# A message-passing layer on one core: node groups inside the message steps, window halves, and a message's last addition on GpSimd

## The chip, the core and the metric

The kernel runs on 1 core of one Trainium2 chip. The metric is the device time in microseconds, the median of 3 runs: 1063.25 us before the change (1062.73 to 1063.36).

## What is computed

50,000 nodes with 128 features, 50,000 edges sorted by target node, 32 edge types, 8 base matrices:

```python
h = jnp.maximum(_layernorm(x, axis=-1), 0.0)
W_rel = jnp.einsum('rb,bdf->rdf', w_comp, weight)
seg = etype * n_nodes + dst
agg = jax.ops.segment_sum(h[src] * norm, seg, num_segments=n_rels * n_nodes)
agg = agg.reshape(n_rels, n_nodes, d_in)
node_repr = jnp.einsum('rnd,rdf->nf', agg, W_rel)
node_repr = node_repr + h_bias + h @ loop_weight
return x + jax.nn.relu(node_repr)
```

The kernel works edge by edge. The message of an edge is its source's row, normalised and multiplied with all eight bases, with the eight products weighted by the type's row of `w_comp` times the edge's weight. A node's result is the sum of its edges' messages, plus bias and its own row times the loop weight.

## The kernel before, in words

It has two stages, one after the other. All engine programs are written out by hand, instruction by instruction, with semaphores between them; each engine's queue keeps its order.

**The message stage** has 98 steps. Each takes one group of 4 tiles of 128 edges (`G = 4`). GpSimd gathers the source rows by indirect DMA (`gathers`, L482). VectorE and ScalarE share the normalisation's statistics (L959, L967; L579, L586). ScalarE applies the relu (L627), TensorE transposes the rows into `hT_ps` (L741), ScalarE copies them to `hT` (L647). One step later TensorE makes the products of each tile with the eight bases, as a high half (L713, bases 4 to 7) and a low half (L719, bases 0 to 3), 512 columns each. `y_ps` holds three tiles of two PSUM banks each. ScalarE scales three of the eight products into `z` (L564, L568), GpSimd adds two of these to `u` (`add_pair`, L431), VectorE adds the other five products in two chains, `sum_b` (`sum_high`) and `sum_a` (`sum_low`, both through L901), and then makes `msg = sum_a + sum_b` (`message`, L934). A bank is free for the next tile when its chain is done (waits on `s_b` and `s_a` in `products`). SyncE stores the group's messages to `msgs` in HBM (L341).

**The node stage** has 98 groups of 4 windows of 128 nodes. SyncE loads 192 message rows for each window into `seg`, two to a partition (`load_windows`, L363). GpSimd loads the nodes' own rows to `xw` (L532) and subtracts the window's first node from the edges' targets (`relative`, `rel`, L450). VectorE makes from `rel` the one-hot matrices `pick`, 96 x 1024 elements for a group (`picks`, L983), the statistics (L994, L1008) and the last step `res` (L1140). ScalarE applies the relu (`hw`, L596) and copies the transposed rows (`hwT`, L604). TensorE transposes (L752) and adds up three products for each window (L786, L787, L789). The node stage's banks are those that the message stage used. Some preparation for the first four groups lies in the message stage already (`early_windows`, SyncE's loads from step 44).

If a window had more than 192 edges, or the edges weren't sorted, a slower branch (`compact`) would run; the trace of before doesn't enter it.

## Time and profile before

| | |
|---|---|
| median of 3 runs | 1063.25 us |
| the profiled execution's own time | 1063.62 us |
| its span, first to last instruction | 1061.8 us |
| granted TensorE clock | 1.000 of full speed |
| busy: TensorE, VectorE, ScalarE, GpSimd | 98%, 96%, 87%, 75% |
| message stage | to about 754 us |
| node stage | from about 754 us to 1058 us |

The profile's page gives first each engine's busy time, then slices of the span, the DMA queues, the chain of work that ended last, the groups of instructions and the DMA issues. The chain that ended last is TensorE for 96% of the span. A view of stretches gives busy times between two moments; a timeline gives starts and lengths. The length of an instruction's record holds its latency, so the pace at which instructions follow each other is read from the distance of their starts. TensorE's fp32 matmul is two instructions, and rows of it say x2.

### The profile page before, as it was taken

Reading aid. Unit: us, or ns where it says so; the run is one execution under the profiler, and the core shown is the slowest. Engines: PE = TensorE matmul, PEld = TensorE weight load, DVE = VectorE, ACT = ScalarE, POOL = GpSimd, SP = SyncE. Lnnn points to the kernel's source line nnn. Section 1 sums busy time; section 2 is a strip of 40 time slices with the busy share of each in tenths; the row PEclk is TensorE's granted clock in tenths of the full one; section 3 lists DMA queues with packets and bytes.
Section 4 is the critical chain, followed back from the end, with each engine's and each line's share of the span. In section 5 each row is a group of like instructions: output and inputs, shape, how many; then the busy total and the mean of one; then the engine's idle time right before and its main releaser. Section 6 shows DMA issues by size and latency. Waiting matters only on the chain.

```text
span 1061.8 us, 23589 instructions
## 1 busy us (share of the span) xinstructions
PE 1044.9 (98%) x4903; PEld 664.7 (63%) x4903; DVE 1018.1 (96%) x4370; ACT 925.6 (87%) x3252; POOL 791.9 (75%) x1282
## 2 busy tenths in 40 slices
PE   5999999999999999999999999999999999999998
PEld 2444444444444444444444444444799999999998
DVE  6999999999999999999999999999999999999996
ACT  6899999999999999999999999999588888888885
POOL 6888888888888888888888888886455555555550
PEclk9999999999999999999999999999999999999999
DMA  3323232323232545232322323222599999999994
GB/s 101 99 75 83 79 92 76 89 70 103 68 93 67 127 117 139 65 93 71 90 78 81 81 77 89 72 76 69 156 299 309 290 300 288 305 293 296 299 303 130
DMA packets 134980, 150.97 MB, mean 142 GB/s; under 512 B 18722, under 2 KB 107970, under 8 KB 134834
## 3 DMA queue, kind: packets, MB, share of 16 engines
q1 hardware_dynamic: 112978, 97.38, 30.6%
q0 software_dynamic: 20384, 51.32, 18.9%
q10 hardware_dynamic: 1472, 0.74, 0.3%
q14 instruction: 106, 0.87, 0.3%
q8 instruction: 40, 0.66, 0.3%
HBM read 97.88 MB, written 51.49 MB: 141 GB/s over the span
## 4 chain that ended last, share of the span: by engine, by line
PE 96%; POOL 2%; issue 1%; DVE 1%; DMA 0%; ACT 0%; POOLq 0%
PE y_ps L719 31%; PE y_ps L713 31%; PE y_ps L789 8%; PE y_ps L786 8%; PE y_ps L787 8%; PE hT_ps L741 4%; PE hT_ps L752 2%; PE mix_ps L752 2%; POOL xg L482 2%; PE mix_ps L735 1%; DMA src_all<-src 0%; DVE pick L983 0%; POOL u L431 0%; ACT hw L596 0%; DVE sum_a L901 0%
## 5 line engine op out<-in xcount | busy, mean ns | idle before, releaser
L482 POOL DMA_INDIRECT xg<-x,idx x392 | 389.2, 993 | 75.5 <-issue 48.9
L719 PE MATMUL y_ps<-w_all,hT 128*128 128x512 f32 x784 | 401.5, 594 | 0.5 <-DVE sum_a L901 0.5
L713 PE MATMUL y_ps<-w_all,hT 128*128 128x512 f32 x784 | 401.6, 594 | 0.0
L568 ACT ACTIVATE z<-y_ps,mix 128x128 f32<-128x128 f32 x784 | 245.0, 364 | 58.6 <-PE y_ps L719 41.7
L719 PEld LDWEIGHTS y_ps<-w_all,hT 128*128 128x128 f32 x784 | 148.8, 190 | 189.8 <-issue 180.9
L901 DVE SCALAR_TENSOR_TENSOR sum_b<-y_ps,mix,sum_b 128x128 f32<-128x128 f32 x784 | 265.5, 339 | 0.0
L713 PEld LDWEIGHTS y_ps<-w_all,hT 128*128 128x128 f32 x784 | 141.5, 191 | 140.5 <-issue 122.1
L431 POOL TENSOR_TENSOR u<-z 128x128 f32<-128x128 f32 x392 | 182.0, 464 | 37.6 <-ACT z L568 28.9
L596 ACT ACTIVATE hw<-xw,shift,nrstd 128x128 f32<-128x128 f32 x392 | 162.7, 482 | 1.7
L532 POOL DMA_DIRECT2D xw<-x x90 | 69.3, 770 | 124.0 <-DVE res L1140 124.0
L786 PE MATMUL y_ps<-w_loop,hwT 128*128 128x128 f32 x782 | 151.1, 274 | 0.0
L789 PE MATMUL y_ps<-seg,pick 97*128 97x128 f32 x782 | 151.1, 274 | 0.0
L787 PE MATMUL y_ps<-seg,pick 96*128 96x128 f32 x782 | 151.1, 274 | 0.0
L901 DVE SCALAR_TENSOR_TENSOR sum_b<-y_ps,mix,z 128x128 f32<-128x128 f32 x392 | 134.3, 343 | 14.1 <-ACT z L564 9.4
L564 ACT ACTIVATE z<-y_ps,mix 128x128 f32<-128x128 f32 x392 | 140.7, 359 | 3.9 <-PE y_ps L713 3.4
L627 ACT ACTIVATE h<-xg,neg_mean 128x128 f32<-128x128 f32 x392 | 135.5, 401 | 0.1
L901 DVE SCALAR_TENSOR_TENSOR sum_a<-y_ps,mix,u 128x128 f32<-128x128 f32 x392 | 133.7, 341 | 1.6 <-POOL u L431 1.4
L901 DVE SCALAR_TENSOR_TENSOR sum_a<-y_ps,mix,sum_a 128x128 f32<-128x128 f32 x392 | 133.6, 341 | 1.6 <-DVE sum_b L901 0.9
L983 DVE TENSOR_TENSOR pick<-iota_n,rel 96x1024 f32<-96x1024 f32 (+2 forms) x107 | 119.0, 1113 | 0.0
L786 PEld LDWEIGHTS y_ps<-w_loop,hwT 128*128 128x128 f32 x782 | 118.3, 191 | 0.5 <-issue 0.5
L787 PEld LDWEIGHTS y_ps<-seg,pick 96*128 96x128 f32 x782 | 118.4, 191 | 0.0
L789 PEld LDWEIGHTS y_ps<-seg,pick 97*128 97x128 f32 x782 | 118.3, 190 | 0.0
(93 smaller groups left out, 1400.5 us busy)
## 6 DMA issues: line engine op xcount, KB each, us to landing
seg<-msgs SPq DMA_DIRECT2D x391, 96.8 KB
msgs<-msg SPq DMA_DIRECT2D x98, 258.0 KB
xw<-x POOLq DMA_DIRECT2D x97, 256.0 KB, 5.0
out<-res SPq DMA_DIRECT2D x97, 256.0 KB, 4.6
type_bc<-type_rows SPq DMA_DIRECT2D x56, 112.0 KB
xg<-x,idx POOLq DMA_INDIRECT x392
w_all<-weight ACTq DMA_DIRECT2D x1, 512.0 KB
dst_i<-dst ACTq DMA_DIRECT2D x1, 196.0 KB, 2.5
```

What stands on the lines that cost most here:

```text
L431: nc.gpsimd.tensor_tensor(u[:, r, :], z[:, r, 0, :], z[:, r, 1, :], ALU.add).then_inc(s_u, 1)
L482: nc.gpsimd.indirect_dma_start(xg[:, q, j, :], None, x, bass.IndirectOffsetOnAxis(ap=idx[:, q, j:j + 1], axis=0)).then_inc(s_gather[q * G ...
L564: nc.scalar.activation(z[:, r, 2, :], y_ps[r][:, B // 2, :], ACT.Copy, scale=mix[:, q, j, B // 2:B // 2 + 1]).then_inc(s_z_high, 1)
L568: ins = nc.scalar.activation(z[:, r, b, :], y_ps[r][:, b, :], ACT.Copy, scale=mix[:, q, j, b:b + 1])
L596: return nc.scalar.activation(hw[:, r, j, :], xw[:, q, j, :], ACT.Relu, bias=shift[:, r, j:j + 1], scale=nrstd[:, r, j:j + 1])
L627: nc.scalar.activation(h[:, q, j, :], xg[:, q, j, :], ACT.Relu, bias=neg_mean[:, q, j:j + 1]).then_inc(s_relu, 1)
L713: nc.tensor.matmul(y_ps[r][:, B // 2:B, :], hT[:, q, j, :], w_all[:, B // 2:B, :], start=True, stop=True).then_inc(s_y_high, 1)
L719: nc.tensor.matmul(y_ps[r][:, 0:B // 2, :], hT[:, q, j, :], w_all[:, 0:B // 2, :], start=True, stop=True).then_inc(s_y, 1)
L786: nc.tensor.matmul(y, hwT[:, r, j, :], w_loop[:, :], start=True, stop=False)
L787: nc.tensor.matmul(y, pick[:, r, j, 0, :][0:SEG_P], seg[0:SEG_P, q, j, 0, 0:F], start=False, stop=False)
L789: mm = nc.tensor.matmul(y, pick[:, r, j, 1, :][0:SEG_P + 1], seg[0:SEG_P + 1, q, j, 1, 0:F], start=False, stop=True)
L901: return nc.vector.scalar_tensor_tensor(out=acc, in0=y_ps[r][:, base, :], scalar=c[:, base:base + 1], in1=first, op0=ALU.mult, op1=ALU.add)
```

## The change

The node groups move into the message stage's steps. Step g works on edge group g and also on node groups behind it: SyncE loads the message rows of node group g - 4, GpSimd loads own rows (g - 4) and makes `rel` (g - 8), VectorE makes the statistics (g - 5), reciprocal and shift (g - 6), `pick` (g - 8) and `res` (g - 9), ScalarE the relu (g - 7), one tile behind each tile of messages, and the copy (g - 8), TensorE the transposes (g - 8) and the sums (g - 9). There are 107 steps: 98 with edges and 9 more for the last node groups.

A window is now two halves of 64 nodes. Each half has its own 104 message rows, one to a partition, so that `pick` has 104 x 512 elements for a group in place of 96 x 1024, and `seg` 208 rows for a window in place of 192. A half's product has 64 stationary columns and writes 64 of the 128 PSUM partitions; there are still twelve matmuls of 128 moving columns for a group, first the four with `w_loop`, then the eight halves.

The PSUM banks are given out anew: five banks in a ring of halves of tiles for the message products (2.5 tiles in place of 3), one for the node sums, and one for both kinds of transposes.

The last addition, `msg = sum_a + sum_b`, moves from VectorE to GpSimd, which makes it two tiles behind its `add_pair`. `sum_a` and `sum_b` have four tiles in place of three.

The table of first rows and the test for the slower branch are made anew, by some 20 small VectorE instructions in steps 1 to 9 and 18 to 19. The slower branch now works out all nodes again at the end.

TensorE, from a step's first tile to the transposes before its fourth, before (`y_ps` with its buffer; L713 and L719 are a tile's two halves):

```order
L713 MATMUL y_ps1<-w_all,hT 128x512
L719 MATMUL y_ps1<-w_all,hT 128x512
L713 MATMUL y_ps2<-w_all,hT 128x512
L719 MATMUL y_ps2<-w_all,hT 128x512
L713 MATMUL y_ps0<-w_all,hT 128x512
L719 MATMUL y_ps0<-w_all,hT 128x512
L735 MATMUL mix_ps<-w_mix,hotT 128x32
L741 MATMUL hT_ps<-ident,h 128x128 x4
```

and now (L752 and L756 are the halves, L762 the node group's transposes, L767 and L770 its sums, L814 those of the messages):

```order
L752 MATMUL y_ps2<-w_all,hT 128x512
L756 MATMUL y_ps3<-w_all,hT 128x512
L762 MATMUL hT_ps<-ident,hw 128x128 x4
L752 MATMUL y_ps4<-w_all,hT 128x512
L756 MATMUL y_ps0<-w_all,hT 128x512
L767 MATMUL win_ps<-w_loop,hwT 128x128 x4
L770 MATMUL win_ps<-seg,pick 64x128 x8
L752 MATMUL y_ps1<-w_all,hT 128x512
L756 MATMUL y_ps2<-w_all,hT 128x512
L806 MATMUL mix_ps<-w_mix,hotT 128x32
L814 MATMUL hT_ps<-ident,h 128x128 x4
```

Between the first tile's products and the second's now stand the node group's transposes, between the second's and the third's the twelve products of the group before it; in the stage of before they stood behind the 98th step.

GpSimd, one step, before (with what each instruction waits for):

```order
L472 COPY idx<-src_all 128x4 [waits s_gather7]
L482 DMA xg<-x,idx 128x128 [waits s_relu,s_idx]
L431 TENSOR_TENSOR u<-z 128x128 [waits s_z]
L482 DMA xg<-x,idx 128x128
L431 TENSOR_TENSOR u<-z 128x128 [waits s_z]
L482 DMA xg<-x,idx 128x128
L444 TENSOR_TENSOR gain<-norm_all,rstd 128x4 [waits s_mix,s_rstd]
L431 TENSOR_TENSOR u<-z 128x128 [waits s_z]
L482 DMA xg<-x,idx 128x128
L431 TENSOR_TENSOR u<-z 128x128 [waits s_z]
L436 CAST msg<-dst_c 128x4 [waits s_stored2]
```

and the later two thirds of a step now:

```order
L491 TENSOR_TENSOR u<-z 128x128 [waits s_z]
L499 TENSOR_TENSOR msg<-sum_a,sum_b 128x128 [waits s_a]
L552 DMA xg<-x,idx 128x128
L512 TENSOR_TENSOR gain<-norm_all,rstd 128x4 [waits s_mix,s_rstd]
L491 TENSOR_TENSOR u<-z 128x128 [waits s_z]
L499 TENSOR_TENSOR msg<-sum_a,sum_b 128x128 [waits s_a,s_stored0]
L552 DMA xg<-x,idx 128x128
L491 TENSOR_TENSOR u<-z 128x128 [waits s_z]
L499 TENSOR_TENSOR msg<-sum_a,sum_b 128x128 [waits s_a]
L504 CAST msg<-dst_c 128x4 [waits s_stored1]
L530 DMA xw<-x 128x4x128 [waits n_res]
L521 TENSOR_TENSOR rel<-seg,half_off 104x8 [waits n_pick,n_seg4]
```

Behind each `u` there is now a `msg`, and at the step's end the load of own rows and `rel`, which waits for the message rows of its group (`n_seg`).

The core of the diff:

```diff
+SUMS = 4
...
-CHUNKS = 2
+HALVES = 2
...
+XRING = 8
+SRING = 6
+HRING = 2
+HALF = P // 2
+SEG_P = 104
+AHEAD = 3
+X_AT = 4
+SEG_AT = 4
+REL_AT = 8
+STATS_AT = 5
+STD_AT = 6
+RELU_AT = 7
+TURN_AT = 8
+SUMS_AT = 9
+OUT_AT = 8
...
+        y_ps = [psum(f"y_ps{b}", [P, B // 2, F]) for b in range(5)]
+        win_ps = psum("win_ps", [P, G, F])
         hT_ps = psum("hT_ps", [P, G, P])
         mix_ps = psum("mix_ps", [P, 512])
 
-        free_first, free_next = (NT - 3) % RING, (NT - 2) % RING
-        win_ps = [y_ps[free_first][:, 0:G, :], y_ps[free_first][:, G:2 * G, :],
-                  y_ps[free_next][:, 0:G, :], y_ps[free_next][:, G:2 * G, :]]
-        hwT_ps = [hT_ps[:, :, :], mix_ps[:, :].rearrange("p (t e) -> p t e", t=G)]
+        def product(t, base):
+
+            high = base >= B // 2
+            return y_ps[(2 * t + (0 if high else 1)) % 5][:, base % (B // 2), :]
...
+            def load_windows(k):
+                windows, q = windows_of(k), k % SRING
+                if k == 0:
+                    sp.wait_ge(s_start, 1)
+                    sp.wait_ge(s_front_st, 16)
+                last = min(k + AHEAD, NG) - 1
+                for g in range(max(0, last - RING + 1) if k == 0 or last == NG - 1 else last, last + 1):
+                    sp.wait_ge(s_stored[g % RING], 16 * (g // RING + 1))
+                if k >= SRING:
+                    sp.wait_ge(n_y, k - SRING + 1)
                 _, rows = nc.values_load_multi_w_load_instructions(
-                    table[0:1, bass.ds(g * G, windows)], (mybir.EngineType.SP,), min_val=0, max_val=ROWS - SEG,
-                    skip_runtime_bounds_check_because="first_row is clamped to EP - SEG or counts compacted rows")
+                    row_tab[0:1, bass.ds(k * G, windows)], (mybir.EngineType.SP,), min_val=0, max_val=ROWS - SEG,
+                    skip_runtime_bounds_check_because="a window's row is clamped to the rows of the edges")
                 for j, row in enumerate(rows):
-                    sp.dma_start(seg[0:SEG_P, q, j, :, :].rearrange("p c f -> p (c f)"),
-                                 msgs[bass.ds(row, SEG), :].rearrange("(p c) f -> p (c f)", c=CHUNKS)
-                                 ).then_inc(done, 16)
-
-            for g in range(NG):
-                store_messages(g, g // RING, g % RING)
+                    sp.dma_start(seg[0:SEG_P, q, j, :, :],
+                                 msgs[bass.ds(row, SEG), :].rearrange("(c p) f -> p c f", c=HALVES)
+                                 ).then_inc(n_seg[q], 16)
...
+            def message(t):
+                g, j = t // G, t % G
+                q, v = g % RING, t % SUMS
+                if j == 0 and g >= RING:
+                    pool.wait_ge(s_stored[q], g // RING * 16)
+                pool.wait_ge(s_a, 2 * t + 2)
+                nc.gpsimd.tensor_tensor(msg[:, q, j, 0:F], sum_a[:, v, :], sum_b[:, v, :], ALU.add).then_inc(s_msg, 1)
...
+                    if 4 <= g and (g - 3) * G + j - 2 < NT:
+                        message((g - 3) * G + j - 2)
+                    if g == 3 and j >= 2:
+                        message(j - 2)
+                if 2 <= g < NG + 2:
                     if is_before(g, 3):
                         pool.wait_ge(s_dst_c, 16)
                     dst_column(g - 2, round_before(n, q, 2), (q - 2) % RING)
-                early_windows(g)
-
-            sweep(pool, NG, gathers)
-            gathers(NG, NG // RING, NG % RING)
-            for g in range(EARLY, EARLY + 2):
-                ask_x(g)
-            gathers(NG + 1, (NG + 1) // RING, (NG + 1) % RING)
-            for g in range(EARLY + 2, LRING):
-                ask_x(g)
+                if node_group(g, X_AT) is not None:
+                    load_x(g - X_AT)
+                if node_group(g, REL_AT) is not None:
+                    relative(g - REL_AT)
+
+            sweep(pool, NGW + REL_AT, gathers)
...
+                if node_group(g, STD_AT) is not None:
+                    window_std(g - STD_AT)
+                if node_group(g, TURN_AT) is not None:
+                    window_hT(g - TURN_AT)
+                window(0)
                 mixing(1)
-                normalised(range(G // 2, G))
+                if here:
+                    normalised(range(G // 2, G))
+                window(1)
...
+                window(2)
                 if not beyond(g, NG - 1):
                     group_means(g + 1, round_after(n, q), (q + 1) % RING)
                 mixing(3)
                 if not beyond(g, NG - 1):
                     group_squares(g + 1, (q + 1) % RING)
-                early_windows(g)
+                window(3)
...
             def products(g, q, j):
-                r = (q * G + j) % RING
-                reused = not is_before(g, 1) or j >= RING
-                if reused:
-                    pe.wait_ge(s_b, g * (3 * G) + 3 * (j - RING + 1))
-                nc.tensor.matmul(y_ps[r][:, B // 2:B, :], hT[:, q, j, :], w_all[:, B // 2:B, :],
+                t = g * G + j
+                if t >= 3:
+                    pe.wait_ge(s_a, 2 * (t - 2))
+                nc.tensor.matmul(y_ps[2 * t % 5][:, :, :], hT[:, q, j, :], w_all[:, B // 2:B, :],
                                  start=True, stop=True).then_inc(s_y_high, 1)
-                if reused:
-                    pe.wait_ge(s_a, g * (2 * G) + 2 * (j - RING + 1))
-                elif j == RING - 1:
+                if t >= 2:
+                    pe.wait_ge(s_b, 3 * (t - 1))
+                nc.tensor.matmul(y_ps[(2 * t + 1) % 5][:, :, :], hT[:, q, j, :], w_all[:, 0:B // 2, :],
+                                 start=True, stop=True).then_inc(s_y, 1)
+
+            def window_transposes(k):
+                pe.wait_ge(n_h, k + 1)
+                for j in range(windows_of(k)):
+                    mm = nc.tensor.transpose(hT_ps[:, j, :], hw[:, k % HRING, j, :], ident[:, :])
+                mm.then_inc(n_hT, 1)
+
+            def sums(v, q, windows):
+                for j in range(windows):
+                    nc.tensor.matmul(win_ps[:, j, :], hwT[:, v, j, :], w_loop[:, :], start=j == 0, stop=False)
+                for j in range(windows):
+                    for c in range(HALVES):
+                        mm = nc.tensor.matmul(win_ps[:, j, :][c * HALF:(c + 1) * HALF],
+                                              pick[:, v, j, c, :][0:SEG_P + 1], seg[0:SEG_P + 1, q, j, c, 0:F],
+                                              start=False, stop=j == windows - 1)
+                return mm
+
+            def window_sums(k):
+                if k == 0:
+                    pe.wait_ge(s_loop, 16 * 3)
                     pe.wait_ge(s_meta, 1)
-                nc.tensor.matmul(y_ps[r][:, 0:B // 2, :], hT[:, q, j, :], w_all[:, 0:B // 2, :],
-                                 start=True, stop=True).then_inc(s_y, 1)
+                pe.wait_ge(n_hT_sb, k + 1)
+                pe.wait_ge(n_pick, k + 1)
+                if k > 0:
+                    pe.wait_ge(n_res, k)
+                sums(k % HRING, k % SRING, windows_of(k)).then_inc(n_y, 1)
...
                 messages(0)
+                if node_group(g, TURN_AT) is not None:
+                    window_transposes(g - TURN_AT)
                 messages(1)
+                if node_group(g, SUMS_AT) is not None:
+                    window_sums(g - SUMS_AT)
                 messages(2)
...
+            def one_hot_rows(v, r, windows):
+                shape = [SEG_P, windows * HALVES, HALF]
+                return nc.vector.tensor_tensor(
+                    pick[0:SEG_P, v, 0:windows, :, :].rearrange("p j c n -> p (j c) n"),
+                    iota_n[0:SEG_P, 0:HALF].unsqueeze(1).to_broadcast(shape),
+                    rel[:, r, 0:windows, :].rearrange("p j c -> p (j c)").unsqueeze(2).to_broadcast(shape),
+                    ALU.is_equal)
...
                     dve.wait_ge(s_bn, g * (2 * DV) + (2 * DV + 2 * j + 1))
-                if past:
-                    message(*b, bj)
...
+                if node_group(g, SUMS_AT) is not None:
+                    window_results(g - SUMS_AT)
...
+                if node_group(g, STD_AT) is not None:
+                    window_shift(g - STD_AT)
+                if node_group(g, STATS_AT) is not None:
+                    window_means(g - STATS_AT)
+                if node_group(g, TURN_AT) is not None:
+                    window_rows(g - TURN_AT)
```

## Rows read from the trace of the kernel before

**Rows 1.** The page, part 1: busy us, share of the span and instructions
```profile
PE 1044.9 (98%) x4903; PEld 664.7 (63%) x4903; DVE 1018.1 (96%) x4370; ACT 925.6 (87%) x3252; POOL 791.9 (75%) x1282
```

**Rows 2.** Stretches: window, length, busy and count of each engine, PEclk, DMA share, GB/s
```profile
400.00:500.00 100.00, 100.00 (x296) 48.83 (x295) 97.83 (x440) 92.57 (x366) 85.12 (x152) 1.00 0.34 92
900.00:1000.00 100.00, 100.00 (x900) 100.00 (x900) 96.76 (x385) 81.57 (x193) 55.69 (x65) 1.00 1.03 297
```

**Rows 3.** Timeline, TensorE, one message step: start us, length us, instruction
```profile
407.57 1.02 PE L713 MATMUL y_ps<-w_all,hT 128*128 128x512 f32 x2
...
414.44 0.30 PE L735 MATMUL mix_ps<-w_mix,hotT 128*128 128x32 f32 x2
...
415.05 1.02 PE L713 MATMUL y_ps<-w_all,hT 128*128 128x512 f32 x2
```

**Rows 4.** Timeline, TensorE, one node group
```profile
816.30 0.60 PE L752 MATMUL mix_ps<-ident,hw 128*128 128x128 f32 x4
816.74 0.39 PE L786 MATMUL y_ps<-w_loop,hwT 128*128 128x128 f32 x2
...
819.42 0.60 PE L752 MATMUL hT_ps<-ident,hw 128*128 128x128 f32 x4
```

**Rows 5.** Timeline, ScalarE behind the last tile of a step
```profile
400.95 1.02 PE L719 MATMUL y_ps<-w_all,hT 128*128 128x512 f32 x2
...
402.01 0.63 ACT L568 ACTIVATE z<-y_ps,mix 128x128 f32<-128x128 f32 x2 [0.29 <-PE y_ps L719]
...
402.52 0.40 ACT L586 ACTIVATE h<-xg,neg_mean 128x128 f32<-128x128 f32 x1
...
403.30 0.48 ACT L596 ACTIVATE hw<-xw,shift,nrstd 128x128 f32<-128x128 f32 x1
```

**Rows 6.** Timeline, TensorE, 128 stationary columns, then one
```profile
14.65 1.11 PE L741 MATMUL hT_ps<-ident,h 128*128 128x128 f32 x4 [0.54 <-ACT h L627]
15.70 1.49 PE L700 MATMUL y_ps<-bin_count,ones 128*1 128x400 f16 x4
```

**Rows 7.** Timeline, GpSimd, one message step
```profile
463.69 0.98 POOL L482 DMA_INDIRECT xg<-x,idx  x1 [0.27 <-POOL idx L472]
464.70 0.46 POOL L431 TENSOR_TENSOR u<-z 128x128 f32<-128x128 f32 x1
...
470.03 0.45 POOL L431 TENSOR_TENSOR u<-z 128x128 f32<-128x128 f32 x1 [0.21 <-issue]
470.43 0.27 POOL L436 CAST msg<-dst_c 128x4 f32<-128x4 int32 x1
...
471.17 0.98 POOL L482 DMA_INDIRECT xg<-x,idx  x1 [0.27 <-POOL idx L472]
```

**Rows 8.** Groups of instructions: busy us, mean ns, idle us before and its cause
```profile
L934 DVE TENSOR_TENSOR msg<-sum_a,sum_b 128x128 f32<-128x128 f32 x392 | 116.3, 297 | 0.0
...
L983 DVE TENSOR_TENSOR pick<-iota_n,rel 96x1024 f32<-96x1024 f32 (+2 forms) x107 | 119.0, 1113 | 0.0
...
L532 POOL DMA_DIRECT2D xw<-x x90 | 69.3, 770 | 124.0 <-DVE res L1140 124.0
```

**Rows 9.** Timeline, the offsets of a group, alone and beside the picks
```profile
754.95 0.25 POOL L450 TENSOR_TENSOR rel<-seg,win_off 96x8 f32<-96x8 f32 x1
...
814.91 1.21 DVE L983 TENSOR_TENSOR pick<-iota_n,rel 96x1024 f32<-96x1024 f32 x1
...
815.16 1.01 POOL L450 TENSOR_TENSOR rel<-seg,win_off 96x8 f32<-96x8 f32 x1
```

**Rows 10.** Timeline, the DMA issues of SyncE, and a wait at the end
```profile
368.10 0.37 SPq L341 DMA_DIRECT2D msgs<-msg  x1
368.98 1.99 SPq L363 DMA_DIRECT2D seg<-msgs  x4
...
1037.19 1.38 SPq L363 DMA_DIRECT2D seg<-msgs  x3
...
1041.15 0.20 POOL L450 TENSOR_TENSOR rel<-seg,win_off 96x6 f32<-96x6 f32 x1 [2.36 <-DMA seg<-msgs]
```

More of the change, by code:

```diff
@@ L352, in load_node_constants @@
                              ).then_inc(s_loop, 16)
                 sp.wait_ge(s_consts, 1)
[L354 to L358 removed]
+                sp.dma_start(pick[SEG_P:SEG_P + 1, :, :, :, :].rearrange("p r j c n -> p (r j) (c n)"),
+                             ones[SEG_P:SEG_P + 1, :].unsqueeze(1).to_broadcast([1, HRING * G, P])).then_inc(s_loop, 16)
@@ L379, in _ @@
+            for r in range(NRING):
+                sp.wait_ge(n_out[r], 16 * sum(x_loads(k) for k in range(r, NGW, NRING)))
             sp.wait_ge(s_table, 16)
             compact = sp.value_load(mode, min_val=0, max_val=1)
-            for q in range(RING):
-                sp.wait_ge(s_stored[q], 16 * len(range(q, NG, RING)))
             with sp.If(compact > 0):
-                with sp.Fori(0, NW + 2) as w:
+                with sp.Fori(0, NW + 3) as w:
                     sp.wait_ge(c_zero, w + 1)
@@ L418, in _, with load_again @@
-            for r in range(NRING):
-                sp.wait_ge(n_out[r], 16 * (len(range(r, NGW, NRING)) + (r == last_g % NRING and LAST_FULL > 0)))
+                def load_again(g):
+                    for j in range(G):
+                        sp.dma_start(seg[0:SEG_P, 0, j, :, :],
+                                     msgs[bass.ds(g * (G * P) + (NODES + j * P + HALF - SEG_P), SEG), :].rearrange(
+                                         "(c p) f -> p c f", c=HALVES)).then_inc(f_load, 16)
@@ L902, in add @@
+            def add(acc, t, c, base, first):
+                return nc.vector.scalar_tensor_tensor(out=acc, in0=product(t, base), scalar=c[:, base:base + 1],
                                                       in1=first, op0=ALU.mult, op1=ALU.add)
@@ L925, in sum_low @@
                     dve.wait_ge(s_a, before)
[L926 to L934 removed]
+                    first = sum_a[:, v, :]
+                add(sum_a[:, v, :], g * G + j, mix[:, q, j, :], base, first).then_inc(s_a, 1)
             def tile_slot(g, n, q, j, more):
@@ L1079, in _, with again @@
             copy_hist()
-            sweep(dve, NG - 1, step, first=1)
-            step(NG - 1, (NG - 1) // RING, (NG - 1) % RING)
+            sweep(dve, STEPS, step, first=1)
             dve.wait_ge(s_table, 16)
             compact = dve.value_load(mode, min_val=0, max_val=1)
-            step(NG, NG // RING, NG % RING)
-            last = NG - 1, (NG - 1) // RING, (NG - 1) % RING
-            sum_low(last[0], last[2], G - 1, 2)
-            sum_low(last[0], last[2], G - 1, 3)
-            message(*last, G - 1)
+            def again(g, loads):
+                dve.wait_ge(f_load, loads)
+                hold(dve, passed["dve"])
+                for j in range(G):
+                    ins = nc.vector.bn_stats(nstats[:, 0, j, :], xw[:, 0, j, :])
+                ins.then_inc(f_dve, 1)
+                dve.wait_ge(f_dve, g * 4 + 2)
+                hold(dve, passed["dve"])
+                for j in range(G):
+                    ins = nc.vector.bn_aggr(nmv[:, 0, j, :], nstats[:, 0, j, :])
+                ins.then_inc(f_mv, 1)
+                nc.vector.tensor_tensor(rel[:, 0, :, :], seg[0:SEG_P, 0, :, :, F], coff[0:SEG_P, :, :],
+                                        ALU.subtract).then_inc(f_dve, 1)
+                dve.wait_ge(f_dve, g * 4 + 3)
+                hold(dve, passed["dve"])
+                nc.vector.tensor_scalar(coff[:, :, :], coff[:, :, :], float(G * P), None, ALU.add).then_inc(f_dve, 1)
+                one_hot_rows(0, 0, G).then_inc(f_pick, 1)
+                dve.wait_ge(f_std, g + 1)
+                hold(dve, passed["dve"])
+                nc.vector.reciprocal(nrstd[:, 0, :], nstd[:, 0, :]).then_inc(f_dve, 1)
+                dve.wait_ge(f_dve, g * 4 + 5)
+                hold(dve, passed["dve"])
+                nc.vector.scalar_tensor_tensor(out=shift[:, 0, :], in0=nmv[:, 0, :, 0], scalar=-1.0,
+                                               in1=nrstd[:, 0, :], op0=ALU.mult, op1=ALU.mult).then_inc(f_shift, 1)
+                dve.wait_ge(f_y, g + 1)
+                hold(dve, passed["dve"])
+                results(0, 0, G).then_inc(f_res, 1)
@@ L1197 @@
     dst_next[0:P - 1, 0] = dst[1:P, 0]
+    dst_far = np.full((P * tiles,), -1, dst.dtype)
+    dst_far[0:inputs["dst"].size - SEG_P] = inputs["dst"].reshape(-1)[SEG_P:]
     w_comp = inputs["L0_gnn_w_comp"]
```

685 lines of the change are left out of this document (321 added, 364 removed).

## The prediction

> **What bounds the kernel now.** I read the page's busy times first, then two stretches, then timelines. The page has TensorE busy for 98% of the span, VectorE for 96%, and GpSimd, with 791.9 us, for 75% [rows 1]. A busy TensorE says little by itself, so the stretches come next: in the middle of the message stage and of the node stage TensorE is busy for all of the 100 us, at the full granted clock, with VectorE at 97.8 and 96.8 us; GpSimd falls from 85.1 to 55.7 us, and the DMA engines rise from a share of 0.34 to 1.03 [rows 2]. The timelines show that TensorE really goes at its pace. A message step starts every 7.48 us (407.57 to 415.05): 6.87 us for the eight half tiles and 0.61 us for the mixing weights and four transposes [rows 3]. A node group takes 3.12 us (816.30 to 819.42): 0.44 us for four transposes, 2.68 us for twelve products, 0.223 us each [rows 4]. 98 x (7.48 + 3.12) = 1039 us, and the rest of the span is the start and the end. So moving node groups between the message steps gains nothing by itself: TensorE has the same work in another order. The time can fall only where TensorE gets less to do, and rises where it has to wait.
>
> **TensorE's sum for a step.** A full step holds both kinds of work: 7.48 + 3.12 = 10.60 us before corrections. There are three.
>
> First, the eight half products of a group. Each has 64 stationary columns and its own half of the PSUM partitions, and two neighbours share no column of the array. No row of before shows two such products. One bound is the pace of the whole ones, 0.223 us each, 1.79 us for eight: nothing gained [rows 4]. The other is that two neighbours run side by side: 0.89 us, a gain of 0.89. I take the second, since nothing in the trace makes disjoint columns wait for each other. The Trainium skill (TensorE: Matmul & The Clock Gate, Part 3: Packing small matmuls) says that products in different column groups run at the same time, and gives 2.38x for three of 32 columns. No row here tests it.
>
> Second, the switch between 128 and 64 stationary columns, twice a step. The nearest rows go from transposes of 128 columns to products with one: the later record starts at 15.70, while the earlier one ends at 15.76 (14.65 + 1.11) [rows 6]. So the array isn't emptied first. I take 0.1 us for each switch, 0.20 a step; the bounds are 0 and 0.26 each, worked out below as a rival.
>
> Third, a new wait. The node group's transposes in TensorE's queue stand behind the step's first tile, and they need all four `hw`. ScalarE makes the last of these at the end of the step before, behind the scaling of the fourth tile and the squares. Today's rows have that chain: the fourth tile's record ends at 401.97, ScalarE's scaling starts at 402.01, the squares at 402.52, the relu at 403.30 and ends at 403.78 [rows 5]. That is 1.81 us after the tile. TensorE issues one more tile meanwhile, 1.72 us (a quarter of 6.87), and is free for the next 0.16 us before a record's end, so 1.56 us after it. With about 0.18 us for the signal and a weight load that no matmul hides, the wait is 0.43 us in each step. Everything of TensorE is queued behind it.
>
> Step: 10.60 - 0.89 + 0.20 + 0.43 = **10.34 us**.
>
> **The other engines in that step.** VectorE loses 116.3 us of `msg` and half of the 119.0 us of `pick` [rows 8]: 1018 - 116 - 60 = 842 us of the whole, 8.6 us a step. ScalarE's work is unchanged. Neither sets the pace. The ring of 2.5 tiles asks that the low sums of a tile are made before TensorE starts the third tile behind it, at least 3.4 us of TensorE's own work later. VectorE is 1.7 us behind a tile now, and with it stays inside.
>
> GpSimd is the close one. Its step of 7.48 us holds 0.21 us of waiting [rows 7], other steps more, so I take 7.2 us of work. Behind an addition the next elementwise instruction starts 0.40 us later (470.03 to 470.43) [rows 7]: four `msg` add 1.6 us. The load of own rows adds 0.77 us [rows 8], `rel` 0.25 us [rows 9]. Sum 9.85 us, 0.5 below TensorE. `rel` takes 1.01 us in place of 0.25 where it meets VectorE's `pick`, and ends with it (815.16 + 1.01 against 814.91 + 1.21) [rows 9]; now there are eight additions a step that can meet a `pick` of half the length. I take 3 us for that over the whole run.
>
> **Start and end.** Steps 3 to 8 have no node sums yet, but GpSimd has its `msg` and loads already: 9.65 us in place of 7.48, six times 2.17 = 13 us lost. From there 90 steps are full (9 to 98), and the last eight node groups run alone at 3.12 us as today. The small VectorE instructions of the table lie in the early steps, where VectorE has room: nothing.
>
> Sum against the profiled execution: 13 + 90 x (10.34 - 10.60) + 3 = -7.4 us, so 1063.6 - 7.4 = 1056.2 us. The median of the runs lies 0.4 us under that execution: **1056 us**. The point at which nothing changes is a step of 10.42 us.
>
> **The rivals.**
> - *Half products one behind the other* (slower). The 0.89 us aren't gained: a step of 11.23 us, or 11.03 if the switches cost nothing, +73 or +55 us; 1127 us in the middle. For it: no row shows two products at once. Chance 0.20.
> - *The array empties at each switch* (slower). A product's record is longer than its pace by 0.16 us, and a weight load that isn't hidden adds about 0.1: 0.26 us twice, a step of 10.66 us, +21 us, 1085 us. Against it speak [rows 6]. The Trainium skill (TensorEngine Tiling (Array Packing), Key Properties) says for this rule that changing the tiling mode drains TensorE. By that rule the time is this one. Chance 0.14.
> - *GpSimd's loop through HBM sets the pace* (slower). `rel` of a step waits for rows that SyncE asks for only when GpSimd's own second `msg` of that step completes an edge group. SyncE's store comes first, 0.88 us later the first load, 1.99 us for the four [rows 10]; the last rows landed 2.6 us behind the last issue (1038.57 to 1041.15) with the DMA engines full [rows 10]. With 0.1 us for the signal that is 5.6 us, and from `rel` to the next such `msg` GpSimd has 4.9 us of work: 10.5 us, more by every microsecond that a landing takes longer with twice the descriptors, and by 1.8 us in every seventh step, whose loads stand behind four of types. It decides from a landing of 2.5 us on. At 10.8 us it is +31 us: 1095 us. Against it: the DMA engines' share is then only about two thirds. Chance 0.17.
> - *Only GpSimd bounds* (faster). If the wait for `hw` and the switches are hidden, TensorE needs 9.71 us and GpSimd 9.85: 13 - 67 = -54 us, 1009 us. Chance 0.10.
> - *The change doesn't do what it says*: a half with over 104 edges would send everything through the slower branch, far beyond this range. 50,000 edges on 50,000 nodes are 64 for a half; I leave it out.
>
> **The numbers.** My own case has 0.39 and the range 1040 to 1072 us, as a step comes out between 10.15 and 10.5 us. The range over all cases is 1030 to 1130 us: it leaves out nearly all of the last case and the top of the first, together under 0.2. About 0.2% (2 us) is what a measurement of this kernel can tell from no change. Faster by more: 0.30 of my own case and the 0.10 of the last, 0.40. Within it: 0.05 of mine and 0.02 of GpSimd's loop, 0.07. Slower: 0.04 of mine, 0.20, 0.14 and 0.15, 0.53. So my likeliest time is a small gain, but the cases on the other side weigh more together.
>
> **What would show it.** In the changed profile: starts of the eight half products 0.11 us apart in place of 0.22 (right), or 0.22 (first rival). The first transposes of a node group with some 0.4 us of idle TensorE before them, released by ScalarE's `hw` (right), or none. A gap at the first half product and at the product behind the last one of 0.1 us or of 0.26. GpSimd's `rel` with waits for `seg` (third rival), or GpSimd waiting for `z`. Steps 3 to 8 starting some 9.6 us apart. The sum is wrong if the bank waits (`s_a`, `s_b`) show in TensorE's idle time, which I priced at nothing, or if steps are regular at a length that none of these gives.

## The result, and the profile after

The changed kernel takes **1172.47 us** (median of 4 runs, 1164.33 to 1175.63), the one before 1062.99 us (4 runs, 1061.93 to 1063.36): a ratio of 1.102, 95% interval 1.0995 to 1.1047. The forecast was 1056 us, with a range up to 1130.

The page of the changed kernel, parts 1 and 4 (busy time; the chain that ended last, by engine):

```profile
PE 1049.5 (90%) x4903; PEld 579.2 (49%) x4903; DVE 942.1 (80%) x3976; ACT 908.4 (77%) x3251; POOL 861.4 (73%) x1674
...
POOL 59%; issue 25%; PE 9%; DVE 3%; ACT 2%; DMA 1%; POOLq 0%; ACTq 0%; DVEq 0%
```

TensorE was busy for 98% [rows 1]. Now no engine is, and the chain, which was TensorE for 96%, is mostly GpSimd and "issue". GpSimd, with 73% busy, is on the chain and yet idle for a quarter of the span, so something in its own queue makes it wait. The stretches say the same (columns as in [rows 2]): none of the five is full in the middle, and the DMA engines aren't either.

```profile
400.00:500.00 100.00, 91.20 (x442) 51.08 (x442) 81.06 (x346) 79.58 (x284) 74.83 (x148) 0.98 0.51 133
900.00:1000.00 100.00, 92.20 (x432) 50.39 (x429) 82.30 (x350) 80.00 (x289) 77.43 (x151) 0.98 0.50 134
```

The waits (engine, instruction and line, what it waited for: us in all, times, the longest):

```profile
DVE sum_a L965 <- POOL u L491: 178.8, 93, 5.4
...
POOL rel L521 <- DMA seg<-msgs: 172.5, 91, 5.2
...
ACT z L600 <- PE y_ps L752: 124.8, 138, 4.0
...
PE y_ps L752 <- DVE sum_a L965: 91.8, 105, 3.5
```

Read from the bottom: TensorE waits for a bank until VectorE has made `sum_a`, VectorE for `u` of GpSimd, and GpSimd does nothing because `rel`, a small instruction of 0.2 us, stands ahead of it and waits for message rows from HBM. One round in the timelines, GpSimd first, then SyncE's issues:

```profile
612.70 0.19 POOL L521 TENSOR_TENSOR rel<-seg,half_off 104x8 f32<-104x8 f32 x1 [1.75 <-DMA seg<-msgs]
...
614.41 0.46 POOL L491 TENSOR_TENSOR u<-z 128x128 f32<-128x128 f32 x1
614.82 0.46 POOL L499 TENSOR_TENSOR msg<-sum_a,sum_b 128x128 f32<-128x128 f32 x1
...
616.84 0.46 POOL L499 TENSOR_TENSOR msg<-sum_a,sum_b 128x128 f32<-128x128 f32 x1
...
621.53 0.80 POOL L530 DMA_DIRECT2D xw<-x  x1
623.60 0.20 POOL L521 TENSOR_TENSOR rel<-seg,half_off 104x8 f32<-104x8 f32 x1 [1.26 <-DMA seg<-msgs]
```

```profile
617.32 0.38 SPq L382 DMA_DIRECT2D msgs<-msg  x1
618.53 1.90 SPq L414 DMA_DIRECT2D seg<-msgs  x4
```

`rel` starts at 612.70. The second `msg` behind it ends at 617.30 and completes an edge group. SyncE's store follows at 617.32 and the four loads at 618.53. The last one is issued at 620.43, and at 623.60 the next `rel` can start. That `rel` belongs to exactly these loads: 10.9 us from one `rel` to the next, whatever the engines have to do. From the `rel` at 301.13 us to the one at 439.44 there are twelve such distances: ten go from 10.43 to 11.73 us, and two are 14.05 and 14.21, where four loads of edge types stand ahead of the `seg` loads; their mean is 11.5.

A load doesn't need the rows that the store just ahead of it writes. In `load_windows` the loads of node group k wait for the store of edge group k + 2 (`AHEAD = 3`), but with `SEG_AT = 4` they stand in SyncE's queue behind the store of edge group k + 4. It is SyncE's order, and not the data, that ties them to GpSimd's last messages. (No run put the loads ahead of the store within a step.)

What this does to VectorE and TensorE:

```profile
614.90 0.35 DVE L965 SCALAR_TENSOR_TENSOR sum_a<-y_ps,mix,u 128x128 f32<-128x128 f32 x1 [1.76 <-POOL u L491]
```

```profile
604.41 2.08 PE L752 MATMUL y_ps<-w_all,hT 128*128 128x512 f32 x2 [2.93 <-DVE sum_a L965]
...
618.69 1.10 PE L752 MATMUL y_ps<-w_all,hT 128*128 128x512 f32 x2 [0.36 <-DVE sum_a L965]
```

### The profile page after: what moved, and what is told of

Read it like the earlier page. It is cut to its first block, busy times and chain, and to the rows that moved or that the text cites. A ratio compares the mean times of both kernels' runs of the same rounds, so it can differ in the third digit from the quotient of the medians.

```text
span 1172.5 us, 23681 instructions
## 1 busy us (share of the span) xinstructions
PE 1049.5 (90%) x4903; PEld 579.2 (49%) x4903; DVE 942.1 (80%) x3976; ACT 908.4 (77%) x3251; POOL 861.4 (73%) x1674
## 4 chain that ended last, share of the span: by engine, by line
POOL 59%; issue 25%; PE 9%; DVE 3%; ACT 2%; DMA 1%; POOLq 0%; ACTq 0%; DVEq 0%
POOL xg L552 26%; POOL msg L499 12%; POOL u L491 11%; POOL xw L530 5%; PE y_ps L752 3%; PE y_ps L756 2%; PE win_ps L770 2%; PE win_ps L767 2%; POOL gain L512 2%; POOL rel L521 1%; POOL idx L542 1%; POOL msg L504 1%; DVE sum_a L965 1%; ACT z L604 1%; DVE res L1076 1%
## 5 line engine op out<-in xcount | busy, mean ns | idle before, releaser
L752 PE MATMUL y_ps<-w_all,hT 128*128 128x512 f32 x784 | 433.0, 635 | 92.2 <-DVE sum_a L965 91.8
L756 PE MATMUL y_ps<-w_all,hT 128*128 128x512 f32 x784 | 409.5, 605 | 0.0
L756 PEld LDWEIGHTS y_ps<-w_all,hT 128*128 128x128 f32 x784 | 152.5, 195 | 194.3 <-issue 174.1
L752 PEld LDWEIGHTS y_ps<-w_all,hT 128*128 128x128 f32 x784 | 121.7, 194 | 205.7 <-issue 141.0
L638 ACT ACTIVATE hw<-xw,shift,nrstd 128x128 f32<-128x128 f32 x391 | 189.6, 489 | 0.0
L499 POOL TENSOR_TENSOR msg<-sum_a,sum_b 128x128 f32<-128x128 f32 x392 | 181.2, 462 | 0.1
L521 POOL TENSOR_TENSOR rel<-seg,half_off 104x8 f32<-104x8 f32 x98 | 19.4, 198 | 180.5 <-DMA seg<-msgs 172.5
L767 PEld LDWEIGHTS win_ps<-w_loop,hwT 128*128 128x128 f32 x782 | 103.6, 194 | 54.9 <-issue 50.6
L767 PE MATMUL win_ps<-w_loop,hwT 128*128 128x128 f32 x782 | 106.0, 279 | 9.3 <-DVE pick L1063 8.0
L770 PE MATMUL win_ps<-seg,pick 105*64 105x128 f32 x1564 | 110.6, 284 | 0.0
L1041 DVE BATCH_NORM_STATS2 nstats<-xw 128x6 f32<-128x128 f32 x391 | 105.0, 269 | 0.0
L770 PEld LDWEIGHTS win_ps<-seg,pick 105*64 105x64 f32 x1564 | 86.3, 139 | 12.2 <-issue 0.9
L1076 DVE SCALAR_TENSOR_TENSOR res<-win_ps,xw 128x512 f32<-128x512 f32 x98 | 66.4, 678 | 21.8 <-PE win_ps L770 21.8
```

The costliest lines, as they stand in the source:

```text
L499: nc.gpsimd.tensor_tensor(msg[:, q, j, 0:F], sum_a[:, v, :], sum_b[:, v, :], ALU.add).then_inc(s_msg, 1)
L638: ins = nc.scalar.activation(hw[:, v, j, :], xw[:, q, j, :], ACT.Relu, bias=shift[:, r, j:j + 1], scale=nrstd[:, r, j:j + 1])
L752: nc.tensor.matmul(y_ps[2 * t % 5][:, :, :], hT[:, q, j, :], w_all[:, B // 2:B, :], start=True, stop=True).then_inc(s_y_high, 1)
L756: nc.tensor.matmul(y_ps[(2 * t + 1) % 5][:, :, :], hT[:, q, j, :], w_all[:, 0:B // 2, :], start=True, stop=True).then_inc(s_y, 1)
L767: nc.tensor.matmul(win_ps[:, j, :], hwT[:, v, j, :], w_loop[:, :], start=j == 0, stop=False)
L770: mm = nc.tensor.matmul(win_ps[:, j, :][c * HALF:(c + 1) * HALF], pick[:, v, j, c, :][0:SEG_P + 1], seg[0:SEG_P + 1, q, j, c, 0:F], start= ...
```

## The experiments

**First: is it the loop?** Each step the loop closes once: SyncE's loads of node group k stand behind the store of edge group k + 4, GpSimd completes that group with the second `msg` of its step k + 8, and at the end of the same step it reaches the `rel` of node group k. Two edits give it a step more of slack, one on each side.

```diff
-SEG_AT = 4
+SEG_AT = 3
```

> Edit: SyncE asks for the message rows of node group g - 3 in step g, in place of g - 4: one step more for them to land before GpSimd's rel. Theory (the loop through HBM sets the pace): the 172.5 us in which rel waited for seg go nearly all, steps fall from some 11.3 us to 10.0 to 10.4, 1050 to 1085 us in all. Rival (the ring of 2.5 tiles and GpSimd's late u set the pace, the wait at rel only takes up slack): GpSimd's idle time moves to u or elsewhere, over 1140 us.

Measured: 1074.94 us, ratio to before 1.011 (1.0084 to 1.0136).

```diff
-REL_AT = 8
+REL_AT = 9
```

> Edit: GpSimd makes rel of node group g - 9 in step g in place of g - 8, the loads stay where they are: the same step more for the rows, given on the other side. Theory (loop through HBM): as good as asking earlier, within 1%, since only the distance between load and rel counts; 1050 to 1090 us. Rival (what helped in asking earlier was the place of the loads in SyncE's queue): no gain here, over 1140 us. VectorE's pick then has its rel one step later, about one step before it needs it.

Measured: 1072.05 us, ratio 1.0094 (1.0072 to 1.0116). Either constant alone takes about 100 us off (97.5 and 100.4), with not one instruction less. GpSimd's waits in e1_load_early:

```profile
POOL rel L521 <- DMA seg<-msgs: 10.3, 3, 4.9
```

172.5 us in 91 waits have become 10.3 in 3. Starts of TensorE's mixing product (L806) are 10.40 us apart there (601.66, 612.06).

**Second: the message back on VectorE**, with the loads where the change put them and with the loads a step early.

```diff
 pool:
-                    if 4 <= g and (g - 3) * G + j - 2 < NT:
-                        message((g - 3) * G + j - 2)
...
 dve, tile_slot:
...
+                if past:
+                    message(*b, bj)
```

> Edit on the changed kernel: the last addition of a message goes back to VectorE, right behind its last sum, as before the change. Theory (loop through HBM): the loop has 1.8 us less work of GpSimd, and the message is ready about two tiles earlier, so rel's waits shrink by 2 us a step or more: 1060 to 1110 us. Rival (VectorE's load was what GpSimd was to take away): VectorE with 0.8 us more a step has 9.5 us, and the time stays or rises, 1160 us or more.

> Both edits: rows asked for one step earlier, and the addition on VectorE. Theory: with the loop open, the bound is TensorE at about 10.1 us a step (its plain work 9.6 us and the wait for hw), and GpSimd at 8.2 us or VectorE at 9.5 us lie under it: 1040 to 1070 us, at or below the edit of the loads alone. Rival (VectorE becomes the bound and the addition is better on GpSimd): slower than the edit of the loads alone by 1% or more.

Measured: 1064.7 us (ratio 1.0017, 1.0003 to 1.0032) and 1065.07 us (1.0022, 1.0004 to 1.004). With `msg` out of GpSimd's queue the loop is open (`rel` waits 31.1 us in 20 times in place of 172.5), and the earlier load adds nothing. The loop needs both parts: the message behind `rel` in one queue, and loads without slack. Against e1_load_early, GpSimd's additions cost 10 us more than VectorE's. Nearly all of it lies before the node sums begin: the six steps from the third L806 on take 57.8 us with them (33.81 to 91.64) and 49.1 without (33.51 to 82.57). From there on the steps are 10.40 us in both.

**Third: do the half products run side by side?** The sum rested on it, and no row of before showed it.

```diff
-                for j in range(windows):
-                    for c in range(HALVES):
+                for c in range(HALVES):
+                    for j in range(windows):
```

> Edit on e1_load_early (1074.94 us, step 10.40 us): the sixteen instructions of a node group's neighbour sums are issued with all first halves ahead of all second halves, so that neighbours in the order write the same 64 columns; same count, sizes and operands. If the two halves run side by side only because they alternate between column groups (my reading: 16 instructions take 1.03 us where 16 one after the other at the step's own weight of a half, 0.223 / 2 = 0.11 us each, would take 1.8), the sums take some 0.8 to 0.9 us more in each of 98 groups: about 1150 to 1160 us. If a half of 64 columns is simply cheap by itself, or if the order of issue does not matter, the time stays at 1075 us within 3 us.

Measured: 1120.74 us, 45.8 above e1_load_early. The sixteen instructions, and what follows them, in e1_load_early and then with neighbours on the same columns:

```profile
608.23 1.05 PE L767 MATMUL win_ps<-w_loop,hwT 128*128 128x128 f32 x8
609.21 1.10 PE L770 MATMUL win_ps<-seg,pick 105*64 105x128 f32 x16
610.24 1.12 PE L752 MATMUL y_ps<-w_all,hT 128*128 128x512 f32 x2
611.20 1.02 PE L756 MATMUL y_ps<-w_all,hT 128*128 128x512 f32 x2
```

```profile
601.67 1.58 PE L770 MATMUL win_ps<-seg,pick 105*64 105x128 f32 x16
603.19 1.13 PE L752 MATMUL y_ps<-w_all,hT 128*128 128x512 f32 x2
```

1.03 us against 1.52, for the same instructions. So alternating between column halves is worth 0.49 us a group, 44 us over 90 steps, which is nearly the whole difference. But the same-column order is still under the 1.79 us of eight whole products: a product of 64 columns takes 0.03 us less even so. The expectation of 0.8 to 0.9 us was too high, since it gave all of the gain to the overlap. (The Trainium skill, TensorE: Matmul & The Clock Gate, Part 3: Packing small matmuls, has products in different column groups at the same time. The runs agree, with 1.5 times for two of 64 columns in fp32.)

**Fourth: the wait for `hw`.** With the loop open, TensorE's one regular wait is the predicted one. e1_load_early, transposes of a node group:

```profile
604.85 1.02 PE L756 MATMUL y_ps<-w_all,hT 128*128 128x512 f32 x2
606.02 0.66 PE L762 MATMUL hT_ps<-ident,hw 128*128 128x128 f32 x4
606.51 1.02 PE L752 MATMUL y_ps<-w_all,hT 128*128 128x512 f32 x2
```

```profile
605.48 0.49 ACT L638 ACTIVATE hw<-xw,shift,nrstd 128x128 f32<-128x128 f32 x1
```

The half tile before is followed after 0.86 us everywhere else, here after 1.17, when `hw` has ended (605.97). TensorE's row shows no idle time there, since the record before it is 1.02 us long and covers most of the wait. The rows of TensorE's weight loads (PEld) show it, in 91 groups:

```profile
PEld hT_ps L762 <- ACT hw L638: 88.3, 91, 1.9
```

The weight loads would be idle for a part of that time anyway, so the cost is taken from the distance of the starts: 0.31 us a step. ScalarE's order is changed:

```diff
+                window(3)
                 mixing(3)
                 if not beyond(g, NG - 1):
                     group_squares(g + 1, (q + 1) % RING)
-                window(3)
```

> Edit on e1_load_early: ScalarE works the fourth tile of a node group (hw) ahead of the message tile's last z and of the squares instead of behind them, about 1.8 us earlier, so that the array's four transposes of hw no longer wait for it (0.31 us in each of some 90 steps of 10.40). If the array's own sum (10.40 less 0.31, 10.09 us) is what is left, 28 us come off: 1047 us, which is faster than both kernels. If GpSimd, with its 9.5 us of work and its waits for z, is already as near, or if z comes later to VectorE because hw goes first, it stays within 5 us of 1075.

> The same move on e4_both (1065.07 us; message on VectorE, loads a step early). By the array's sum, the step goes from 10.40 to 10.09 us: 1037 us. If VectorE, which has 9.8 us of work in a step here, and its waits for z bound instead, the gain is under 10 us: 1055 or more.

Measured: 1042.55 us (ratio 0.9822, 0.9802 to 0.9841) and 1033.42 us (0.9733, 0.9718 to 0.9747). The steps are 10.03 us in both, which is TensorE's own sum. One line moved is worth 32 us, and both are faster than either kernel. Message on GpSimd or on VectorE makes no difference in a full step; the 9 us between the two are the first steps again (the same six take 57.9 against 49.2 us).

**Fifth: the tail.** The last node groups stand alone. In the changed kernel:

```profile
1142.56 1.10 PE L770 MATMUL win_ps<-seg,pick 105*64 105x128 f32 x16
1143.59 0.66 PE L762 MATMUL hT_ps<-ident,hw 128*128 128x128 f32 x4
1145.94 1.22 PE L767 MATMUL win_ps<-w_loop,hwT 128*128 128x128 f32 x8 [1.70 <-DVE pick L1063]
1147.09 1.98 PE L770 MATMUL win_ps<-seg,pick 105*64 105x128 f32 x16
```

VectorE makes `res` of a group, the statistics, and then `pick` of the next group, all between one group's sums and the next. There is a second cause: part of the tail runs at a lower granted clock (1.98 us for the same sixteen instructions that took 1.10). It is priced below. The edit, in VectorE's step:

```diff
+                ahead = g > NG + 1 and node_group(g, TURN_AT) is not None
+                if ahead:
+                    window_rows(g - TURN_AT)
                 if node_group(g, SUMS_AT) is not None:
                     window_results(g - SUMS_AT)
...
-                if node_group(g, TURN_AT) is not None:
+                if node_group(g, TURN_AT) is not None and not ahead:
                     window_rows(g - TURN_AT)
```

> e7_both_relu_first, and in the last steps, where no message tile is left, VectorE makes the next group's one-hot rows (pick) ahead of the results instead of behind them. In the tail the array waits for pick 1.0 to 1.7 us in each of eight groups (e4_both), since results, statistics and pick follow one another. If that order is the cause, 8 to 12 us come off e7_both_relu_first; if the tail is bound by the round through ScalarE (std, hwT, four relu) or by the loads, under 3 us.

Measured: **1027.76 us** (1026.48 to 1028.68, 5 runs), ratio 0.9674 (0.9661 to 0.9687): 5.7 us less than e7_both_relu_first, where 8 to 12 were expected. The waits for `pick` are down to one. Others take their place, as `hw`:

```profile
1007.59 0.66 PE L750 MATMUL hT_ps<-ident,hw 128*128 128x128 f32 x4 [0.46 <-ACT hw L626]
...
1010.97 0.66 PE L750 MATMUL hT_ps<-ident,hw 128*128 128x128 f32 x4 [0.80 <-ACT hw L626]
```

**Sixth: is GpSimd's work as a whole the bound?** SyncE issues the load of own rows (`load_x`) in GpSimd's place.

```diff
 sp:
                 if node_group(g, SEG_AT) is not None:
                     load_windows(g - SEG_AT)
+                if node_group(g, X_AT - 2) is not None:
+                    load_x(g - X_AT + 2)
...
 pool:
-                if node_group(g, X_AT) is not None:
-                    load_x(g - X_AT)
...
```

> Edit on the changed kernel (1172.47 us) alone: SyncE issues the load of a node group's features (xw) behind the four segment loads, instead of GpSimd (0.80 us of its time in each of 98 steps). In the loop msg, store, loads, rel this load stands on GpSimd between the last message and rel, where GpSimd waits anyway (1.3 to 1.8 us behind it). If the loop sets the step, the wait of rel only grows by 0.8 us and the time stays within 10 us of 1172. If GpSimd's work as a whole set the step, up to 78 us would come off. Since the early steps, before the loop closes, are bound by GpSimd (9.8 us), the few of them that have such a load may give 2 or 3 us.

> The same move on e8_tail_rows_first (1027.76 us), where the array is busy 97% of the span. If the array bounds the steady steps, only early steps gain: 1024 to 1028. If the load collides on SyncE's queue with stores and segment loads and makes rel late, it is slower, up to 1040.

Measured: 1195.36 us, and 1036.77 us (ratio 0.9754). The first, by its waits:

```profile
POOL rel L534 <- DMA seg<-msgs: 249.7, 87, 6.9
```

GpSimd lost 78 us of work (97 issues of 0.80) and its wait for `seg` grew by 77: work that lies inside a wait is worth nothing. That the time rose by 23 us I had not expected. The loads land later, 3.66 us behind the last issue (median of 68 waits in the timelines) in place of 3.26 (of 74), now that the own rows go through the same queue. From one `rel` to the next the median is 11.45 us in place of 10.97 in steps without loads of types, which is that much more. On the fastest version the move costs 9 us. The steps are 10.14 us in place of 10.03; why, I haven't shown.

**Seventh: why is the trip through HBM longer than in the kernel before?** There a load went to 96 partitions, now it goes to 104. Two other counts, on the changed kernel; at 96 also on the fastest version. No half of the input has more than 92 edges.

```diff
-SEG_P = 104
+SEG_P = 96
```

> The changed kernel (1172.47 us) with 96 message rows for a half in place of 104 (SEG_P 96; no half of the input has more than 92 edges). A load then goes to 96 partitions, as in the kernel before, whose last rows landed 2.6 us behind the last issue against 3.2 to 3.3 now. Three theories of that difference, inside a loop whose length is the step's: (a) the number of partitions must divide well over the DMA engines: 96 does, 104 doesn't, so the landing falls back to 2.6, the step by 0.5 to 0.6 and the time by about 50 us, 1125. (b) The bytes set it: 8% fewer, 0.1 to 0.2 us, 1155 to 1165. (c) A landing's fixed part or the traffic of the gathers sets it: within 5 us of 1172.

> The same with 112 rows, which is more bytes than 104 but again a multiple of 16. By (a), the count of partitions, the time falls to about 1130 to 1140 though 8% more is loaded. By (b), the bytes, it rises, 1180 to 1190. By (c) it stays within 5 us of 1172.

> e8_tail_rows_first (1027.76 us) with 96 rows for a half. TensorE is busy for 97% of the span there and its products keep their 128 columns, so a faster load can only help in the tail, where GpSimd waits 15.5 us for rows in four waits: 1022 to 1028 by every theory. A lower time than 1020 would mean that the loads bound more than the trace shows.

Measured: 96 rows 1121.07 us (ratio 1.0552, 1.0536 to 1.0569), 112 rows 1143.63 us (1.0776, 1.0753 to 1.0799), and the fastest version with 96 rows 1027.63 us, unchanged. More bytes than 104, and 29 us faster. The trip at 112 rows, SyncE's issues and then the `rel` that waits for them:

```profile
622.93 0.37 SPq L382 DMA_DIRECT2D msgs<-msg  x1
623.87 1.88 SPq L414 DMA_DIRECT2D seg<-msgs  x4
```

```profile
629.36 0.20 POOL L521 TENSOR_TENSOR rel<-seg,half_off 112x8 f32<-112x8 f32 x1 [1.41 <-DMA seg<-msgs]
```

From the store to the first load it is 0.94 us here, 0.93 with 96 rows, and 1.21 with 104. From the last issue to `rel` the medians are 3.17, 2.93 and 3.26 us. So the trip is 0.36 us shorter with 112 rows and 0.61 with 96; over some 90 steps that is 32 and 55 us, and 29 and 51 were measured. Theory (a) is right for the time between store and load. In the landing 112 rows gain less than 96, so something else has a part there, perhaps the bytes; what it is isn't shown. The time with 112 rows came out 4 us above the 1130 to 1140 that the theory gave. (The Trainium skill, DMA: Bandwidth & Descriptors, Why a DMA increments its semaphore by 16 and not by 1, says that such a copy is spread over the largest number of engines up to 16 that divides both sides' slowest dimension. By it 104 rows would use 13 engines, 96 and 112 all 16. The times agree with that, and so does a count on the page of the profile, below.)

The line on DMA packets, with 104 rows, with 96 and with 112:

```profile
DMA packets 177886, 154.46 MB, mean 132 GB/s; under 512 B 17573, under 2 KB 150877, under 8 KB 177741
...
DMA packets 172803, 151.23 MB, mean 135 GB/s; under 512 B 18746, under 2 KB 145794, under 8 KB 172658
...
DMA packets 185316, 157.69 MB, mean 138 GB/s; under 512 B 18747, under 2 KB 158307, under 8 KB 185171
```

The rows themselves are packets of 516 B. Of the packets under 512 B there are 1173 more with 96 rows and 1174 more with 112, and each kernel has 391 loads of `seg`: three small packets a load more than with 104 rows, as many as 16 is more than 13. No view gives the packets by engine, so the number of engines is read from this count and not seen.

## Why the prediction was wrong

**The step that failed is the choice of what bounds.** I took TensorE's sum of 10.34 us for the step and gave GpSimd's loop through HBM a chance of 0.17. The step was the loop's, 11.5 us. The loop is worth 98 to 100 us, by e1_load_early and e2_rel_late. I had written it down with its right parts, at 10.8 us, and set it aside with "the DMA engines' share is then only about two thirds". The share is 0.51, and yet the loads land later (3.26 us) than the 2.6 us of before, which come from a stretch (1037 to 1041 us) with a share of 0.96 [rows 10]. Idle DMA engines didn't shorten the landing.

**The loop's own terms** were 0.1 + 0.88 + 1.99 + 2.6 us and 4.9 us of work, 10.5 in all. The round shown above has 0.02 + 1.21 + 1.90 + 3.17 and 4.60, 10.9. Two were too small. The trip was priced with the rows of loads to 96 partitions [rows 10], and the change makes it 104. That explains the first: with 96 rows it is 0.93. It explains about half of the second: with 96 rows the landing is 2.93, and why it isn't 2.6 no run shows. The steps with loads of types were priced at 1.8 us more and show 3: in the one of 14.05 us the first load starts 2.99 us behind the store (349.38 to 352.37), which is the 1.8, but the landing takes 4.51 as well. So 10.8 us became 11.5 (L806 from 105.11 to 1117.23, 88 steps). That is 63 us over 90 steps, and with the 14 us of the tail below it takes the rival's 1095 us to 1172. My range ended at 1130. (The 31 us of that rival leave out the 3 us for GpSimd's collisions with `pick` that my own sum has.)

**TensorE's sum was right.** With the loop open the step is 10.40 us, against 10.34. By its terms, from e1_load_early: the eight half tiles 6.88 (6.87 forecast), mixing and transposes 0.61 (0.61), the wait for `hw` 0.31 and 0.05 of longer transposes behind it (0.43), the node group's transposes 0.44 (0.44), the four loop products up to the first half 0.98 (0.89 and 0.1 for the switch), the eight halves 1.03 (0.89), and 0.10 at the switch back (0.96 from 610.24 to 611.20 in place of 0.86; 0.1). Products and switches are 2.11 us against 2.68 before [rows 4]: 0.57 saved, where 0.89 less 0.20 was forecast. The rivals of serial halves and of an array emptied at each switch fall: the two switches cost 0.19 us, not 0.52, and the serial rival's 1.79 us for the halves is 1.03. (The rule of TensorEngine Tiling (Array Packing), Key Properties, in the Trainium skill, that changing the tiling mode drains TensorE, is not borne out at the price that I gave it, 0.26 us a switch; whether the 0.09 and 0.10 us are such a drain, no row shows.)

**GpSimd.** 9.85 us a step was forecast (the terms add up to 9.82), 9.64 are there (10.90 less the wait of 1.26). It isn't the bound of full steps: e9_x_on_sync and e10_best_x_on_sync take work off and gain nothing. In the first steps it is, and these came nearly as forecast: some are 9.64 us apart (43.62, 53.26, 62.88) against 9.65, and all six together take 58.9 us against 57.9.

**VectorE.** 842 us of work were forecast, 942.1 are there and 892.1 in e1_load_early. Most of the 100 us lie in small instructions that last longer than before, as `hotT` with 560 ns in place of 281; why, I haven't shown. It isn't the bound either way. Its `msg` was counted as a relief, and there was nothing to relieve: e4_both, with the message on VectorE, is 10 us faster than e1_load_early, and e7_both_relu_first 9 us faster than e6_relu_first.

**The bank waits**, priced at nothing, are 91.8 us of TensorE's idle time. They are the loop's consequence, through `u` and `sum_a`, not a lack of banks: in e1_load_early 7.6 us are left of them.

**The tail** was priced "at 3.12 us as today". In e1_load_early a group takes about 4.9 us there (seven from 1032.94 to 1067.42): 14 us over eight. Two causes share them. `res` and `pick` follow one another on VectorE between two groups' sums. And three of the groups ran at the lower clock, 6.24 us each, where those behind them, at full clock, took 3.6 to 3.9: an estimate of 7 us, half of the tail's loss. With 5 us for the longer step (90 x 0.06) that is the 19 us by which e1_load_early is over 1056.

In sum: 1056 + 5 + 14 + 98 = 1173 us.

## What to carry to other kernels

When an instruction that waits for a load is put ahead of work that produces the store for the next load, on the same in-order queue, follow the circle round once and add it up; here it set the pace with no engine and no DMA queue full. A load can be part of such a circle without needing the rows of the store ahead of it: its place in the issuing queue is enough. One step of slack on either side opened it, and the rings of buffers were already long enough. And before an engine is relieved, look at which engine's queue a wait will be left in.

Price a transfer by rows of the same shape. Here 8 partitions more cost 51 of the 109 us that were lost, and nothing once the loop was open (e13_best_rows_96).

## What the runs showed of the hardware

- Loads and stores of SyncE: with loads to 96 and 112 partitions the first load started 0.93 and 0.94 us behind the store's start, with 104 only 1.21 us behind, in otherwise equal programs.
- fp32 products of 64 stationary columns: 0.064 us for an instruction when neighbours alternate between the two column halves, 0.095 when they don't (1.03 and 1.52 us for sixteen).
- Behind some waits of TensorE the granted clock was lower, and the wait so cost twice. Two stretches of the changed kernel, behind idle times of 1.70 and 2.93 us, and one of e1_load_early's tail (columns as in [rows 2]):

```profile
1147.00:1150.00 3.00, 3.00 (x21) 2.29 (x20) 0.89 (x3) 0.61 (x2) 0.20 (x1) 0.50 0.63 178
604.00:606.00 2.00, 1.59 (x2) 0.84 (x3) 2.00 (x9) 0.00 (x0) 1.83 (x3) 0.53 0.12 35
...
1033.00:1052.00 19.00, 15.28 (x89) 12.50 (x90) 7.60 (x36) 7.46 (x20) 2.56 (x7) 0.50 0.65 173
```

  0.50 is the lower of the two levels, 1.2 GHz. The sixteen instructions of a node group took 1.98 us there and 1.10 at the upper level, 2.4 GHz. Not every wait did this: in e1_load_early the groups from 1053 to 1068 us had waits of 0.96 to 1.53 us and a granted clock of 0.99. Over the whole span the granted clock was 0.974 of full, against 1.000 before and 0.996 in the fastest version.
